# Running counts added in PSUM, and routing scores scaled in four operations, in a decoder layer on one core

## What is computed

```python
def _L0_ffn_ref(input_features, centroids, ln_g, ln_b, w1, b1, w2, b2):
    E, D, F = (8, 128, 512)
    x = input_features.reshape(-1, D)
    aff = x @ centroids.T
    assign = jnp.argmax(aff, axis=1)
    onehot = jax.nn.one_hot(assign, E, dtype=x.dtype)
    ...
    h = jax.nn.relu(jnp.einsum('etd,efd->etf', xn, w1) + b1[:, None, :])
    y = x[None, :, :] + jnp.einsum('etf,edf->etd', h, w2) + b2[:, None, :]
    alpha = jax.nn.sigmoid(x @ centroids.T)
    ...
    out = jnp.einsum('te,etd->td', onehot, gated)
```

## Time and profile before

| | |
|---|---|
| median of 3 runs | 604.65 us (603.29 to 607.4) |
| the profiled execution | 602.47 us, of which the profile's span is 600.2 us |
| PE busy | 528.8 us, 88% of the span, 7951 instructions |
| DVE busy | 496.4 us, 83%, 1762 instructions |
| ACT busy | 492.7 us, 82%, 1358 instructions |
| POOL busy | 421.1 us, 70%, 820 instructions |
| chain that ended last, by engine | POOL 31%, PE 29%, issue 22%, DVE 10% |
| granted clock of PE | 0.989 of full speed over the span |

### The profile page before, as it was taken

One profiled execution on the slowest core, in us unless ns is written; L12 is line 12 of the kernel. 1 busy time (PEld: TensorE's weight loads), 2 busy tenths in 40 slices (PEclk: granted clock), 3 DMA queues, 4 the chain that ended last, 5 costly groups with the idle time before them and its releaser, 6 DMA issues.

```text
span 600.2 us, 25006 instructions
## 1 busy us (share of the span) xinstructions
PE 528.8 (88%) x7951; PEld 410.0 (68%) x7951; DVE 496.4 (83%) x1762; ACT 492.7 (82%) x1358; POOL 421.1 (70%) x820
## 2 busy tenths in 40 slices
PE   2755999999999988999989999898879998999995
PEld 1533776666666666666666666666668898899994
DVE  3627899999999999999999999999768777777773
ACT  1735788988988888888888888888778797899993
POOL 1311568888888888888888888887757766555553
PEclk9996999999999999999999999999999999999999
DMA  5142112122122111232211211110301222322210
GB/s 150 41 57 52 29 35 63 43 58 55 56 78 88 57 55 56 66 92 63 56 56 57 59 52 39 38 38 22 86 21 56 70 64 72 98 74 67 68 53 14
DMA packets 55183, 35.35 MB, mean 59 GB/s; under 512 B 14977, under 2 KB 50434, under 8 KB 55057
## 3 DMA queue, kind: packets, MB, share of 16 engines
q1 hardware_dynamic: 50160, 24.44, 15.6%
q0 software_dynamic: 4320, 8.66, 4.3%
q10 hardware_dynamic: 576, 0.66, 0.4%
HBM read 24.46 MB, written 9.74 MB: 57 GB/s over the span
## 4 chain that ended last, share of the span: by engine, by line
POOL 31%; PE 29%; issue 22%; DVE 10%; ACT 2%; DMA 2%; DVEq 2%; POOLq 1%; SPq 0%; ACTq 0%
PE side L940 8%; POOL expert_rows L1980 6%; POOL pay L1952 4%; PE quad L925 4%; PE side L925 4%; POOL on L1900 3%; POOL rs_T L1914 3%; POOL x L1923 3%; POOL rs_L L1875 2%; DVE hT L1551 2%; PE side L661 1%; PE quad L909 1%; PE quad L690 1%; DMA mk<-in_mask 1%; POOL ve_L L1873 1%
## 5 line engine op out<-in xcount | busy, mean ns | idle before, releaser
L2013 POOL DMA_INDIRECT out<-yo,rb x71 | 70.1, 987 | 60.1 <-DVE yo L1757 53.8
L1980 POOL DMA_INDIRECT expert_rows<-pay,sli x64 | 65.5, 1024 | 33.9 <-DVE sli L1603 19.6
L1048 ACT ACTIVATE ex<-qk,cf 128x512 f32<-128x512 f32 x128 | 85.4, 721 | 0.1
L1409 DVE TENSOR_REDUCE mx<-quad 128x16 f32<-128x1024 f32 x64 | 77.5, 1219 | 4.5 <-PE quad L690 4.1
L940 PE MATMUL side<-w,hT 128*128 x568 | 76.8, 278 | 4.7 <-DVE hT L1551 3.1
L940 PEld LDWEIGHTS side<-w,hT 128*128 128x128 f32 x568 | 69.1, 192 | 7.6 <-issue 7.3
L1064 ACT ACTIVATE prob<-quad 128x1024 f32<-128x1024 f32 x64 | 65.8, 1032 | 3.0 <-PE quad L728 2.2
L1541 DVE TENSOR_SCALAR xh<-rb 128x128 f32<-128x128 f32 x71 | 25.2, 356 | 28.2 <-issue 23.3
L1088 ACT ACTIVATE xn<-x,mr,rs_T 128x128 f32<-128x128 f32 x64 | 28.1, 486 | 24.3 <-POOL mr L1916 24.1
L1161 ACT COPY w1b<-w 128x512 f32 x71 | 43.5, 615 | 0.3 <-issue 0.3
L1009 ACT ACTIVATE xn<-xin,rs_L 128x128 f32<-128x128 f32 x64 | 22.2, 394 | 24.8 <-POOL rs_L L1875 24.7
(11 more groups left out here) (270 smaller groups left out, 1634.1 us busy)
## 6 DMA issues: line engine op xcount, KB each, us to landing
rb<-expert_rows SPq DMA_DIRECT2D x71, 68.0 KB, 1.9
xin<-in_x SPq DMA_DIRECT2D x32, 128.0 KB, 3.3
cin<-in_ctx SPq DMA_DIRECT2D x32, 128.0 KB, 2.1
xr<-in_x SPq DMA_DIRECT2D x32, 128.0 KB
w<-in_w1t SPq DMA_DIRECT2D x8, 256.0 KB, 3.6
w<-in_w2t SPq DMA_DIRECT2D x8, 256.0 KB, 3.4
out<-yo,rb POOLq DMA_INDIRECT x71
expert_rows<-pay,sli POOLq DMA_INDIRECT x64, 2.9
```

What stands on the lines that cost most here:

```text
L1048: act(ex[g.par][:, i, :, :].rearrange("p a t -> p (a t)"), qk[g.par][:, :, :].rearrange("p a t -> p (a t)"), ACT.Copy, scale=own4[:, i:i + ...
L1409: v.tensor_reduce(mx[g.par][:, 2 * h_:2 * h_ + 2, :], quad[:, 2 * h_:2 * h_ + 2, :].rearrange("p r (h k) -> p r h k", k=SQ), AX.X, ALU.max ...
L1980: v.indirect_dma_start(out=rows, out_offset=bass.IndirectOffsetOnAxis(ap=sli[g.par][:, j:j + 1], axis=0), in_=pay[g.par][:, j, :], in_offs ...
L2013: v.indirect_dma_start(out=o_rows, out_offset=bass.IndirectOffsetOnAxis(ap=number, axis=0), in_=yo[b.c % 4][:, :], in_offset=None, bounds_ ...
```

## The change

Three edits. First, the running counts: `ranks` gets a product of the identity with cnt, broadcast to the three pieces of its bank, ahead of the triangle's product, so that the counts are in PSUM's sum; `place` is gone, `own_rank` reads the ranks from PSUM and multiplies them by the marks, and `counted` becomes a copy of the totals from PSUM. Second, both stand at the turn's start. Third, `scaled_scores` is four operations, one for each of two tiles and two pieces, in place in y1, each with one tensor input and one column of sc; the third piece isn't touched, and `affinities` reads y1. The buffer tm, the third column of sc and POOL's two memsets of it are gone.

```diff
-        sc = two("sc", [P, J, 3])
-        tm = two("tm", [P, J, 3, E])
+        sc = two("sc", [P, J, 2])
...
                 wait(pe, dv_r, g.n, "o")
                 free(g, "ranks")
                 bank_ = at("ranks", g)
+                wait(pe, dv_r, g.n - 1, "tot")
+                mm(bank_[:, 0:(J + 1) * E].rearrange("p (a e) -> p a e", e=E), identf,
+                   cnt[:, :].unsqueeze(1).broadcast_to((P, J + 1, E)), start=True, stop=False)
                 mm(bank_[:, 0:(J + 1) * E], tri_b[:, :], ohb[g.par][:, :, :].rearrange("p j e -> p (j e)"),
-                   start=True, stop=False)
+                   start=False, stop=False)
...
                 wait(dv, dv_t, g.n, "y1")
                 wait(dv, po_t, g.n, "pow2")
-                wait(dv, dv_r, g.n - 2, "af")
-                v.tensor_tensor(tm[g.par][:, :, :, :],
-                                y1[g.par][:, :, D:D + 3 * E].rearrange("p j (a e) -> p j a e", e=E),
-                                sc[g.par][:, :, :].unsqueeze(3).broadcast_to((P, J, 3, E)), ALU.mult
-                                ).then_inc(*dv_r.done("ab"))
+                for j in range(J):
+                    for a in range(2):
+                        own = slice(D + a * E, D + (a + 1) * E)
+                        last = v.tensor_scalar(y1[g.par][:, j, own], y1[g.par][:, j, own], sc[g.par][:, j, a:a + 1],
+                                               None, ALU.mult)
+                last.then_inc(*dv_r.done("ab"))
...
-            def place(g):
-
-                wait(dv, dv_r, g.n - 1, "tot")
-                wait(dv, dv_r, g.n - 2, "sl")
+            def counted(g):
+
                 wait(dv, pe_r, g.n, "rank")
-                v.tensor_tensor(rk[g.par][:, :, :], at("ranks", g)[:, 0:J * E].rearrange("p (j e) -> p j e", e=E),
-                                cnt[:, :].unsqueeze(1).broadcast_to((P, J, E)), ALU.add
-                                ).then_inc(*dv_r.done("rk"))
-
-            def counted(g):
-
-                wait(dv, dv_r, g.n, "rk")
-                v.tensor_tensor(cnt[:, :], cnt[:, :], at("ranks", g)[:, J * E:(J + 1) * E], ALU.add
-                                ).then_inc(*dv_r.done("tot"))
+                v.tensor_copy(cnt[:, :], at("ranks", g)[:, J * E:(J + 1) * E]).then_inc(*dv_r.done("tot"))
...
             def own_rank(g):
 
-                wait(dv, dv_r, g.n, "rk")
-                wait(dv, dv_r, g.n, "o")
-                v.tensor_tensor(rk[g.par][:, :, :], rk[g.par][:, :, :], ohb[g.par][:, 0:J, :], ALU.mult
-                                ).then_inc(*dv_r.done("pr"))
+                wait(dv, dv_r, g.n - 2, "sl")
+                wait(dv, pe_r, g.n, "rank")
+                v.tensor_tensor(rk[g.par][:, :, :], at("ranks", g)[:, 0:J * E].rearrange("p (j e) -> p j e", e=E),
+                                ohb[g.par][:, 0:J, :], ALU.mult).then_inc(*dv_r.done("pr"))
...
             def one(g):
+                stage(g, 8, own_rank)
                 stage(g, 8, counted)
-                stage(g, 8, own_rank)
...
-                stage(g, 7, place)
...
-            for k in range(2):
-                v.memset(sc[k][:, :, 2], 1.0)
```

More of the change, by code:

```diff
@@ L353, in decoder_kernel @@
         dv_t = stage_steps("dve_cross", "x1 | b0 b1 a0 a1 | mt | y1")
-        dv_r = stage_steps("dve_route", "w0 w1 | b0 b1 a0 a1 | ab | af | g | i0 i1 | f | o | al | rk | tot | pr | sl | si")
+        dv_r = stage_steps("dve_route", "w0 w1 | b0 b1 a0 a1 | ab | af | g | i0 i1 | f | o | al | tot | pr | sl | si")
         po_l = stage_steps("pool_norm_x", "eps pow")
@@ L1465, in y_sum @@
                 first(dv, g, s_vec, 1)
-                wait(dv, dv_r, g.n - 2, "ab")
+                wait(dv, dv_r, g.n - 2, "af")
                 wait(dv, ac_t, g.n, "n")
@@ L1502, in affinities @@
                 wait(dv, dv_r, g.n - 2, "i1")
-                v.tensor_reduce(af[g.par][:, :, :], tm[g.par][:, :, :, :].rearrange("p j a e -> p j e a"), AX.X,
+                v.tensor_reduce(af[g.par][:, :, :], y1[g.par][:, :, D:D + 3 * E].rearrange("p j (a e) -> p j e a", e=E), AX.X,
                                 ALU.add).then_inc(*dv_r.done("af"))
@@ L1770, in leftovers @@
                 if c == 1:
-                    own_rank(g28)
                     slots(g28)
@@ L1789, in leftovers @@
                 if c == 8:
-                    place(g29)
+                    own_rank(g29)
                     counted(g29)
-                    own_rank(g29)
                 if c == 9:
@@ L1807, in leftovers @@
                 if c == 19:
-                    place(g30)
+                    own_rank(g30)
                     counted(g30)
-                    own_rank(g30)
                 if c == 20:
@@ L1823, in leftovers @@
                 if c == 25:
-                    place(g31)
+                    own_rank(g31)
                     counted(g31)
-                    own_rank(g31)
                     wait(dv, dv_r, g31.n, "tot")
@@ L1841, in _ @@
             rows_in(Block(2))
+            own_rank(g28)
             counted(g28)
```

## The result

The changed kernel takes 614.35 us (median of 4 runs, 613.16 to 617.74), and the kernel before 604.06 us (4 runs, 603.29 to 607.4). The ratio is 1.0165, with a 95% interval of 1.013 to 1.02: slower by 1.7%.

A forecast was written before the change was run, and what follows sets the result against it. The prediction took POOL's wait for DVE's sli to bound the loop. Loop +9.1, PE +0.5 and experts' stage +0.5 us made +10.1 us; against the 604.65 us median, 614.7 us, range 607 to 620.

The forecast's parts named there:

- The wait: DVE's scores beside POOL's rotation qk: the first of the four is held until qk ends, taking some 0.8 us.
- walk: Step-by-step timing of one group on DVE, from the four scores to sli's end: 241.49 instead of 241.14 us.
- first rival: DVE's four scores aren't held by POOL's qk, so sli ends earlier: 598.7 us; chance 0.10.
- The spacing: DVE's scores start 0.14 us apart, 0.16 where one meets mt; sli starts 1.18 us after the first.
- second rival: DVE's four scores are held but follow 0.07 us apart: 608.8 to 611.2 us; chance 0.15.
- What bounds the loop: In the loop, POOL's first scatter hangs on sli's end: +0.35 us in each of 26 groups, +9.1 us.
- third rival: DVE bounds the loop after all, and 0.5 us a group comes off: 593 us; chance 0.05.
- The counts: DVE's count and marks operations in the loop: some 0.5 us less per group, none on the chain, costed at zero.
- One sign that I had named: In the changed kernel's profile, DVE would wait longer before ont; no size given.
- PE's product: PE's new identity product: 0.18 us each, covered by idle time in the loop, counted three times, +0.5 us.
- fourth rival: PE is pushed over by the product or its wait for the count: up to 5.8 us more, 620 us; chance 0.03.
- The experts' stage: Two late groups' scores on DVE's chain, 0.66 us each until af, less rank addition and wait: +0.5 us together.

The follow-up runs named there:

- e3: Kernel before with sli moved directly behind ont, ahead of the one score operation tm: 600.96 us, ratio 0.9918.
- e8: Changed kernel with the four score operations moved ahead of ont, sli still behind ont: 621.35 us, ratio 1.0281.
- e7: Changed kernel with a constant 0.5 instead of the column of sc in the four score operations: 610.79 us, ratio 1.0087.
- e4: Kernel before with sli written ahead of ont instead of behind the scores: 598.6 us, ratio 0.9906.
- e2: Changed kernel with the one score operation tm put back, so the counts' edit alone: 604.24 us, ratio 0.9993.
- e11: Kernel with the counts' edit alone and tm, POOL's x moved between mt and the first scatter: 612.58 us, ratio 0.9903 (another chip).
- e1: Kernel before with the four score operations in place of tm, counts still added by DVE: 616.03 us, ratio 1.019.
- e12: Counts' edit alone with tm, POOL's x moved between mt and the first scatter, and sli ahead of ont: 615.54 us, ratio 0.9945 (another chip).
- e6: Counts' edit alone with the one score operation tm, and sli moved ahead of ont: 598.22 us, ratio 0.9911.
- e5: Changed kernel with sli moved ahead of ont, so the four score operations stand behind it: 603.78 us, ratio 0.9973.
- e9: Kernel before with POOL's x moved between mt and the first scatter: 612.56 us, ratio 0.9872 (another chip).
- e10: Changed kernel with POOL's x moved between mt and the first scatter: 642.15 us, ratio 1.0359 (another chip).

## Why the prediction was right

**The wait (right).** The prediction's walk put the first operation's end at qk's end, and it ended 0.04 us behind it. That the four are held rests on three sorts of row: the 0.79 us of the first of them, e3's 0.79 us of a 128x2 sli, and e8's 1.32 us, which is the full length of qk. The first rival (not held, 598.7 us) falls by each. The Trainium skill, "SBUF — State Buffer", section "Who interferes with whom", says that tensor_scalar can enter a mode with two ports and then contends with GpSimd, and the rows of after and of e3 agree with it. It gives the ports to whichever issues first; in e8 the held operation starts 0.02 us ahead of qk by the profile, so either that start isn't the issue or the rule doesn't hold there, and no run here tells which.

**The spacing (right, one term small).** The second started 0.70 us behind the first (0.74 in the walk), the third 0.20 later where I had 0.16, the fourth 0.13 and sli 0.14 later (0.14 each). From the first of the four to sli: 1.17 us, predicted 1.18. From sli to the scatter: 0.97 us, as predicted. The second rival (0.07 apart, 608.8 to 611.2 us) falls in after, and e7 shows what it would have taken: with a constant the kernel takes 610.79 us, inside that rival's bounds.

**What bounds the loop (right).** The distance went from 12.63 to 12.98 us, +0.35 as predicted, and 26 of them took +9.14 us against 9.1. The count of 26 needs a correction: on before's chain the step stands at 25 first scatters, and at four of these, the first at 103.11 among them, the chain comes from mt and not from sli. It costs nothing, since from the second group to the 28th every first scatter starts 0.82 us after sli ends, in before and in after. e4 and e3 confirm it from the other side: in the kernel before, ending this wait earlier is worth 0.25 and 0.19 us a group. The third rival (DVE the bound, 593 us) falls by e2, where DVE has 0.30 us less a group to do and nothing moves.

**The counts (zero, right; the sizes off).** The product with the marks, read from PSUM, takes 0.11 us and not the 0.17 I took from the earlier trace rows, although POOL's yg runs beside it:

```profile
241.64 0.11 DVE L1583 TENSOR_TENSOR rk<-side,ohb 128x16 f32<-128x16 f32 x1
...
241.64 0.72 POOL L1929 TENSOR_TENSOR yg<-y,br 128x256 f32<-128x256 f32 x1
```

Against 0.58 us that is as the walk had it. The operations of this part on DVE took 16.6 us in the loop of before (22 additions, 3.6; 22 sums of the count, 2.3; 22 products, 10.7) and take 5.9 in e2 (22 products, 2.5; 22 copies, 3.4), which is the 0.5 us a group that I wrote. But DVE's busy time fell by 0.30 a group only (e2's windows). Neighbouring operations overlap in it and are counted once; where the other 0.2 us lies wasn't followed. None of it is on the path in after. One sign that I had named failed: DVE doesn't wait longer before ont (5.1 us in the loop's window against 5.5 in before). What it saves it waits in its row maxima, for PE: 7.6 us against 1.0.

**PE's product (covered, as predicted; 0.13 and not 0.18).** The product, in two pieces, stands on after's chain three times, at 84, 98 and 422 us. At the first rank it has 0.13 us:

```profile
84.20 0.13 PE side L866 x2
```

The fourth rival (PE pushed over, 620 us) didn't come true in after, but its mechanism is real: in e11, where POOL's wait is gone, the same 0.13 us is on the chain.

**The experts' stage (right in size, in part by luck).** tm's place there is taken by the four, and until af starts they need 478.75 - 478.09 = 0.66 us, the predicted value. But only this one of the two groups stands on after's chain, and PE's product doesn't stand on it there:

```profile
478.09 0.62 DVE L1498 TENSOR_SCALAR y<-y,sc 128x8 f32<-128x8 f32 x4
...
478.75 0.21 DVE L1506 TENSOR_REDUCE af<-y 128x16 f32<-128x48 f32 x1
```

The stage and PE's small terms came to +0.73 us from the 28th group's scatter on, where the sum had +0.5 for the stage and 2 x 0.18 for PE.

**The start (a term that was missing).** The first chained scatter came 2.05 us later, and the sum had up to 0.18 for the way to it. In before it stood 0.66 us behind mt's end, as sli had ended ahead of mt, and in after 1.06 us, as sli ended behind it. The row of after is the first of this text; that of before, in its timeline of POOL:

```profile
103.11 1.08 POOL L1980 DMA_INDIRECT expert_rows<-pay,sli  x1 [0.67 <-issue]
```

These 0.40 us are the price of the four in a group where qk doesn't hold them: e1 has the same wait of 1.05 us there, e2 has 0.67. They are the 27th step beside the 26 periods. The other 1.65 us lie ahead of mt's end. Two products on after's chain make 0.26 us of them at most. The first input takes 4.24 us to land instead of 3.70, in the chains of after and of before:

```profile
0.74 4.24 DMA xin<-in_x
```

```profile
0.74 3.70 DMA xin<-in_x
```

and the granted clock between 20 and 60 us is 0.83 and not 0.87, by windows of after and of before:

```profile
20.00:60.00 40.00, 24.62 (x375) 15.12 (x383) 23.67 (x81) 20.28 (x45) 7.46 (x16) 0.83 0.28 52
```

```profile
20.00:60.00 40.00, 24.35 (x399) 15.04 (x397) 23.58 (x81) 20.74 (x47) 8.22 (x18) 0.87 0.29 50
```

Over all fourteen profiled executions this scatter goes with the granted clock from 0 to 104 us and not with the edits. It stands at 103.11 and 104.53 us where that clock is 0.95 (before, e12), at 105.16 and 105.82 with 0.93 (after, e8), between 104.72 and 105.76 with 0.92 (e2, e4, e6, e7), between 106.11 and 107.48 with 0.90 (e1, e3, e5, e9), and at 109.37 and 110.74 with 0.89 (e11, e10). Before's profile has the highest clock and the earliest scatter of all. So most of the 1.65 us is the spread between executions, and with it a part of the spans' 12.0 us; why the clock differs is open. By the medians of the runs the difference is 10.3 us, beside the predicted 10.1. That these two lie so close is in part luck, for the spread of either kernel's runs is over 4 us.

Where I was wrong is in the experiments. In e4 the issue of a scatter isn't covered by a short operation ahead of it. In e5 the four cost 4.2 us though sli is out of their way. In e9 the distance came out and the time didn't. In e8 and e10 I looked at the operations that I moved and not at what they would then run beside. In e8 the late input was alpha's, and in e10 the cover was itself an operation that holds DVE.

## What to carry to other kernels

When an operation is split or replaced on DVE, whose operations POOL's were seen to hold, ask first which long POOL operation it runs beside and what is queued behind it. Here one held operation became a held one with three behind it, so that sli started 0.43 us later; 0.08 us came back because sli no longer met mt, and the other 0.35 us was paid 26 times, because POOL itself waited for sli. Take a shorter busy time on an engine as a gain only after the trace shows that engine on the chain: 0.3 us a group less on DVE was worth nothing, and moving one operation of 128x2 made the kernel before 0.9% faster. A move that closes a wait shifts the bound to the next engine, and an extra that was free until then (PE's product, 0.13 us) has to be counted again.

## What the runs showed of the hardware

- A DVE tensor_scalar from SBUF to SBUF is held by POOL's elementwise operations qk, x and mt at any size seen here, down to 128x2 (0.79 us beside qk in e3, where it takes 0.16 unhindered). If it starts 0.02 us ahead of POOL's, it is still held for the whole of it (1.32 us in e8). DVE's product of one PSUM and one SBUF tensor wasn't held by such an operation: 0.11 us. Nor is every operation of POOL one that holds: ohb, of two SBUF tensors, took 0.16 or 0.17 us all 18 times that it lay inside the 1.04 us of POOL's power of four columns. These are timelines of DVE and POOL in the kernel before:

```profile
245.70 0.17 DVE L1532 SCALAR_TENSOR_TENSOR ohb<-lead,rank 128x16 bf16<-128x16 f32 x1
...
244.94 1.04 POOL L1952 TENSOR_TENSOR pay<-ve,half 128x4 f32<-128x4 f32 x1
```

- From start to start, DVE's tensor_scalars of 128x8 lie 0.13 us apart with a column of scalars (after) and 0.07 with a constant (e7), where neither is held nor meets mt.
- The first scatter starts 0.82 us after the end of sli when it waits for it (in before, after and e3), 0.53 us after a POOL operation of 0.24 us when it waits for nothing (e4, e6), and 0.16 us after one of 0.74 us (e9).
- The same scatter lasts 1.08 us, or up to 1.25 us in 16 of 27 groups of e5 and 1.21 us in 19 of e9, in both with DVE's sums for pay beside it. What stretches it is open.
